# Gated cross-attention on one Trainium2 core: weights of the first batch split in other slots, from four staging places instead of two

## The reference

```
q = layernorm(x) @ Wq + bq            # 32 heads of 128
k, v = split(ctx @ Wkv + bkv)         # 8 heads of 128 each: four q heads share one
o = softmax(q k^T / sqrt(128)) v
x = x + tanh(g_xattn) * (o @ Wo + bo)
x = x + tanh(g_ffn) * ffn(layernorm(x))   # base matrix + 2 of 8 low-rank experts
```

## Time and profile before

| | us |
|---|---|
| three runs | 2407.01, 2410.34 (median), 2415.13 |
| the profiled execution, time | 2413.21 |
| the profiled execution, span from first to last instruction | 2411.1 |
| busy: TensorE / VectorE / ScalarE / GpSimd | 2305.1 / 1830.4 / 1687.1 / 1623.3 |
| mean granted TensorE clock | 0.984 |
| from one nm reduction to the next in the second batch (850.70, 884.34, 916.18, 950.79, 990.90 us) | 33.64, 31.84, 34.61, 40.11 |
| the same in the first batch (105.43, 147.39, 182.85, 220.53, 260.63 us) | 41.96, 35.46, 37.68, 40.10 |

### The profile page before, as it was taken

One profiled execution on the slowest core, in us unless ns is written; L12 is line 12 of the kernel. 1 busy time (PEld: TensorE's weight loads), 2 busy tenths in 40 slices (PEclk: granted clock), 3 DMA queues, 4 the chain that ended last, 5 costly groups with the idle time before them and its releaser, 6 DMA issues.

```text
span 2411.1 us, 37754 instructions
## 1 busy us (share of the span) xinstructions
PE 2305.1 (96%) x12568; PEld 1972.2 (82%) x12568; DVE 1830.4 (76%) x3167; ACT 1687.1 (70%) x3208; POOL 1623.3 (67%) x1367
## 2 busy tenths in 40 slices
PE   5889899899999999999999999999999999999988
PEld 5778788788888888888888888888888888888764
DVE  5677787778878777786877878787687878778775
ACT  4667676667767777776777777677677767777663
POOL 5687686876657767775776778577666747755652
PEclk9999999999999999999999999999999999999999
DMA  7333332336223233324213333333422222122201
GB/s 253 127 119 126 114 127 100 133 125 213 97 97 100 85 129 107 119 72 171 106 53 121 107 106 112 109 102 105 162 71 88 80 73 86 53 97 71 79 36 53
DMA packets 122591, 258.11 MB, mean 107 GB/s; under 512 B 13344, under 2 KB 46624, under 8 KB 122144
## 3 DMA queue, kind: packets, MB, share of 16 engines
q1 hardware_dynamic: 122400, 255.71, 31.4%
HBM read 188.81 MB, written 66.86 MB: 106 GB/s over the span
## 4 chain that ended last, share of the span: by engine, by line
PE 78%; POOL 7%; DVE 5%; issue 4%; DMA 4%; ACT 1%; SPq 1%; POOLq 0%; ACTq 0%; DVEq 0%
PE psW L350 11%; PE psW L351 11%; PE psW L352 11%; PE psW L533 7%; PE psW L535 7%; PE psW L534 7%; PE psS L350 6%; PE psS L352 6%; PE psS L351 6%; POOL xs L713 2%; DMA stg<-in_wq 2%; PE psW L405 2%; PE psW L413 2%; DVE mrun L1116 2%; PE psW L450 1%
## 5 line engine op out<-in xcount | busy, mean ns | idle before, releaser
L713 POOL TENSOR_TENSOR xs<-xs,mb 128x512 f32<-128x512 f32 (+1 forms) x832 | 1066.6, 1308 | 527.8 <-ACT mb L777 527.8
L1116 DVE TENSOR_TENSOR mrun<-psS,mrun 128x512 f32<-128x512 f32 (+1 forms) x704 | 484.1, 688 | 416.6 <-ACT xs L777 412.2
L777 ACT ACTIVATE xs<-psS 128x512 f32<-128x512 f32 (+1 forms) x832 | 497.6, 598 | 218.1 <-PE psS L352 208.7
L870 ACT ACTIVATE ph<-xs 128x512 fp32r<-128x512 f32 (+1 forms) x832 | 520.6, 626 | 0.0
L928 DVE TENSOR_TENSOR pl<-psP,ph 128x512 fp32r<-128x512 f32 (+1 forms) x674 | 460.9, 684 | 53.6 <-ACT ph L870 47.7
L1140 DVE TENSOR_TENSOR psum_<-psP,psum_ 128x512 f32<-128x512 f32 (+1 forms) x674 | 458.8, 681 | 20.7 <-POOL pl L717 20.7
L867 ACT ACTIVATE psP<-xs 128x512 f32<-128x512 f32 (+1 forms) x674 | 403.5, 599 | 1.7 <-DVE psum_ L1140 1.7
L533 PE MATMUL psW<-ph,vh 128*128 128x512 f32 (+1 forms) x832 | 338.6, 407 | 41.0 <-POOL pl L717 37.3
L350 PE MATMUL psS<-ql,kh 128*128 128x512 f32 (+1 forms) x832 | 345.8, 416 | 3.2 <-DVE mrun L1116 3.2
L535 PE MATMUL psW<-ph,vl 128*128 128x512 f32 (+1 forms) x832 | 330.0, 397 | 0.0
L534 PE MATMUL psW<-pl,vh 128*128 128x512 f32 (+1 forms) x832 | 329.9, 397 | 0.0
(11 more groups left out here) (145 smaller groups left out, 4580.5 us busy)
## 6 DMA issues: line engine op xcount, KB each, us to landing
wqh<-scr_wq SPq DMA_DIRECT2D x96, 256.0 KB, 2.7
wql<-scr_wq SPq DMA_DIRECT2D x96, 256.0 KB, 3.0
woh<-scr_wo SPq DMA_DIRECT2D x48, 512.0 KB, 3.3
wol<-scr_wo SPq DMA_DIRECT2D x48, 512.0 KB, 4.4
stg<-in_wq SPq DMA_DIRECT2D x32, 256.0 KB, 4.2
scr_wq<-wqh SPq DMA_DIRECT2D x32, 256.0 KB, 2.0
scr_wq<-wql SPq DMA_DIRECT2D x32, 256.0 KB, 2.5
stg<-in_wo SPq DMA_DIRECT2D x32, 256.0 KB, 3.2
```

Of the source, the lines that this page charges most:

```text
L713: eng.tensor_tensor(tile, tile, mb[0:rows_of(t), U % 2, :], ALU.subtract).then_inc(s_sub)
L777: return eng.activation(hi, src, ACT.Copy)
L870: eng.activation(ph[0:rows, T % RP, :], xs[0:rows, T % RX, :], ACT.Exp).then_inc(s_h)
L1116: eng.tensor_tensor(run, psS[0:rows, s % 2, :], a, ALU.max).then_inc(s_m)
```

## The change

It touches only what happens up to the end of the first batch. First, `cuts` is written by slots of the head and no longer by the projections; the number of splits is the same:

```
-            if kind == "q" and 2 * n + part + 2 < 2 * NU:
-                cuts[s + 1] += halves("q", 2 * n + part + 2)
-            if kind == "k" and part == 3 and n + 1 < 8:
-                cuts[s + 1] += halves("k", n + 1)
-            if kind == "v" and part == 12 and n + 1 < 4:
-                cuts[s + 1] += halves("v", n + 1)
-            if kind == "o" and part == 1 and n + 1 < NU:
-                cuts[s + 1] += halves("o", n + 1)
...
+    for U in range(NU + 1):
+        at, u = NT * U, U % 4
+        if U + 2 < NU:
+            cuts[at + 7] += halves("q", 2 * U + 4)
+            cuts[at + 8] += halves("q", 2 * U + 5)
+        if u % 2 == 0 and U // 2 + 1 < 8:
+            cuts[at + 9] += halves("k", U // 2 + 1)
+        if u == 3 and U // 4 + 1 < 4:
+            for a in range(2):
+                cuts[at + 9 + a].append(("v", U // 4 + 1, a))
+        if U != 1:
+            for a in range(2):
+                cuts[at + (12 if u == 3 or U == 0 else 13) + a].append(("o", max(U - 1, 0), a))
+        for t in (9, 11) if u == 1 else (11,) if u != 3 or U == 3 else ():
+            if spare:
+                cuts[at + t].append(spare.pop(0))
```

Second, four staging places: the two of stg, and until the last head of the batch the two of pp, which that batch doesn't use otherwise; a fetch may be issued ten slots ahead:

```
+        w = no % 4 if no < n4 else no % 2
+        last = there[w][-1] if there[w] else None
...
-            s = max(s, at - 5, cut_at[no - 2][1] + 1 if no - 2 >= len(first) else 0)
+            s = max(s, at - 10, cut_at[last][1] + 1)
...
+        def staged(no):
+            w = stage[no][0]
+            return stg[:, w, :] if w < 2 else pp[:, w - 2, :]
...
-                if no >= 2:
-                    sp.wait_ge(s_cut, 2 * (no - 1))
+                if last is not None:
+                    sp.wait_ge(s_cut, 2 * (last + 1))
...
+                        else:
+                            act.wait_ge(s_keep["c"], 32 * 16)
```

Third, GpSimd's steps in heads of the first batch:

```
-                "S0,S1 M,S2 L0,S3 S4 S5 S6 S7 S8 S9 S10 S11 S12 -",
+                "S0,S1 M,S2,S3 L0,S4 S5,S6 S7 S8 S9 S10 S11 S12 - - -",
```

```
+        for t, names in enumerate((AT[U % 4] if U else "k1 - k2 v0 q0 k3 q1 v1 - v2 - v3 -").split()):
...
-    jobs[0].append(("k", 0, 2))
...
-            proj_k(0, 1)
...
+                if c == 2:
+                    fetch("v", 0, 0)
+                    fetch("v", 0, 1)
+                    fetch("q", 2, 0)
+            fetch("q", 3, 0)
+            eng.dma_start(acc[:, :, :], x[:, 2:4, :]).then_inc(s_acc, 16)
...
-            upper_ctx(2)
-            upper_k(0, 1)
-            upper_ctx(3)
...
+                if s in (0, 2):
+                    upper_ctx(2 + s // 2)
...
-            lower_ctx(1)
             lower_k(0, 0)
             lower_q(0, 0)
             lower_q(0, 1)
-            lower_ctx(2)
-            lower_k(0, 1)
-            lower_ctx(3)
+            lower_ctx(1)
...
+                if s in (0, 2):
+                    lower_ctx(2 + s // 2)
```

More of the change, by code:

```diff
@@ L62, in gated_block @@
     for U in range(UN + 2):
-        for t, names in enumerate(AT[U % 4].split()):
+        for t, names in enumerate((AT[U % 4] if U else "k1 - k2 v0 q0 k3 q1 v1 - v2 - v3 -").split()):
             for name in names.split(","):
@@ L86, in gated_block @@
     cuts = {s: [] for s in range(SLOTS)}
-    for s in range(SLOTS):
-        for kind, n, part in jobs[s]:
-            if kind == "q" and 2 * n + part + 2 < 2 * NU:
-                cuts[s + 1] += halves("q", 2 * n + part + 2)
-            if kind == "k" and part == 3 and n + 1 < 8:
-                cuts[s + 1] += halves("k", n + 1)
-            if kind == "v" and part == 12 and n + 1 < 4:
-                cuts[s + 1] += halves("v", n + 1)
-            if kind == "o" and part == 1 and n + 1 < NU:
-                cuts[s + 1] += halves("o", n + 1)
-    cuts[0] += halves("q", 2) + halves("q", 3)
-    cuts[9] += halves("o", 0)
-    for n in range(16 * (B - 1)):
-        b, i = divmod(n, 16)
[L101 to L107, removed]
+    cuts[0] += halves("q", 2) + halves("q", 3)
+    spare = [("c", n, 0) for n in range(16)]
+    for U in range(NU + 1):
[14 more added lines that the diff above has]
+                cuts[at + t].append(spare.pop(0))
+    for n in range(16, 16 * (B - 1)):
+        b, i = divmod(n, 16)
+        cuts[NT * (NU * b + 3 + i // 2) + (10, 12)[i % 2]].append(("c", n, 0))
     cut_at = [(p, 0) for p in first] + [(p, s) for s in range(SLOTS) for p in cuts[s]]
@@ L111, in gated_block @@
     fetches = {s: [] for s in range(SLOTS)}
-    s = 0
+    stage, there, s = [], [[] for _ in range(4)], 0
     for no, (p, at) in enumerate(cut_at):
-        if no >= len(first):
-            s = max(s, at - 5, cut_at[no - 2][1] + 1 if no - 2 >= len(first) else 0)
+        n4 = sum(z < NT * (NU - 1) for _, z in cut_at)
+        w = no % 4 if no < n4 else no % 2
+        last = there[w][-1] if there[w] else None
+        stage.append((w, len(there[w]), last))
+        there[w].append(no)
+        if no >= len(first) + 2:
+            s = max(s, at - 10, cut_at[last][1] + 1)
+            assert s <= at, (p, at, s)
             fetches[s].append(p)
@@ L198, in gated_block @@
         s_in = {k: sem("s_in_" + k) for k in ("x", "wk", "c0", "c1", "c2", "c3")}
-        s_stg = [sem("s_stg0"), sem("s_stg1")]
+        s_stg = [sem("s_stg%d" % w) for w in range(4)]
         s_keep = {k: sem("s_keep_" + k) for k in ("q0", "q1", "k", "v", "o", "c")}
@@ L552, in fetch @@
                 no = number[kind, n, a]
-                if no >= 2:
-                    sp.wait_ge(s_cut, 2 * (no - 1))
-                    if order[no - 2][0] == "c":
-                        keep_ctx(order[no - 2][1])
-                        sp.wait_ge(s_keep["c"], 32 * (order[no - 2][1] + 1))
+                w, _, last = stage[no]
+                if last is not None:
+                    sp.wait_ge(s_cut, 2 * (last + 1))
+                    if order[last][0] == "c":
+                        keep_ctx(order[last][1])
+                        sp.wait_ge(s_keep["c"], 32 * (order[last][1] + 1))
                 if kind == "c":
-                    b, k, (lo, w) = n // 16 + 1, n % 4, CW[n // 4 % 4]
-                    eng.dma_start(stg[:, no % 2, 0:w], ctxT[b, :, k, lo:lo + w]).then_inc(s_stg[no % 2], 16)
+                    b, k, (lo, z) = n // 16 + 1, n % 4, CW[n // 4 % 4]
+                    eng.dma_start(staged(no)[:, 0:z], ctxT[b, :, k, lo:lo + z]).then_inc(s_stg[w], 16)
                 else:
-                    eng.dma_start(stg[:, no % 2, :], raw[kind](n, a)).then_inc(s_stg[no % 2], 16)
+                    eng.dma_start(staged(no), raw[kind](n, a)).then_inc(s_stg[w], 16)
             def keep(kind, n):
@@ L608, in _ @@
             eng.dma_start(bkv_sb[:, :], bkv).then_inc(s_c, 16)
+            eng.dma_start(tg[:, 0:1], gx.partition_broadcast(128)).then_inc(s_c, 16)
+            eng.dma_start(tg[:, 1:2], gf.partition_broadcast(128)).then_inc(s_c, 16)
             for c, (lo, w) in list(enumerate(CW))[1:]:
@@ L653, in _ @@
                     eng.dma_start(acc[:, :, :], scr_b[:, 2 * b:2 * b + 2, :]).then_inc(s_acc, 16)
[L654 to L659, removed]
+                if s in (5, 14, 22):
+                    r = (5, 14, 22).index(s) + 1
                     sp.wait_ge(s_bias, 2 * r)
                     eng.dma_start(scr_b[:, 2 * r:2 * r + 2, :], acc[:, :, :]).then_inc(s_sb, 16)
+                if s in (7, 16, 24):
+                    r = (7, 16, 24).index(s) + 1
+                    sp.wait_ge(s_sb, 16 * r)
+                    r = (r + 1) % 4
+                    eng.dma_start(acc[:, :, :], x[:, 2 * r:2 * r + 2, :]).then_inc(s_acc, 16)
                 if s == TN - 21:
@@ L686, in cut @@
                 no = number[kind, n, a]
-                raw = stg[:, no % 2, :]
+                raw = staged(no)
+                w, before, _ = stage[no]
                 if kind == "c":
-                    w = CW[n // 4 % 4][1]
-                    raw = raw[:, 0:w]
-                    hi, lo = cst[:, 0:w], raw
+                    z = CW[n // 4 % 4][1]
+                    raw = raw[:, 0:z]
+                    hi, lo = cst[:, 0:z], raw
                     if n:
@@ L702, in cut @@
                         pool.wait_ge(s_keep[name], 32 * i)
-                pool.wait_ge(s_stg[no % 2], 16 * (no // 2 + 1))
+                pool.wait_ge(s_stg[w], 16 * (before + 1))
                 eng.tensor_scalar(hi, raw, 1.0, 0.0, ALU.mult, ALU.add).then_inc(s_cut)
@@ L750, in _ @@
                     eng.tensor_scalar(xraw[:, :], xraw[:, :], tg[:, 0:1], None, ALU.mult).then_inc(s_bob)
-                if s in (4, 12, 20, 27):
-                    r = (s // 8 + 1) % 4
+                if s in (4, 13, 21, 28):
+                    r = (4, 13, 21, 28).index(s) + 1
                     pool.wait_ge(s_bob, 1)
-                    pool.wait_ge(s_acc, 16 * (s // 8 + 1))
-                    if r:
+                    pool.wait_ge(s_acc, 16 * r)
+                    if r < 4:
                         pool.wait_ge(s_bs, 2 + 2 * r)
@@ L902, in _ @@
```

(14 more changed lines are left out.)

2 lines of the change are left out of this document (1 added, 1 removed).

## The result

The changed kernel takes 2351.88 us (median of four runs, 2350.98 to 2352.85), the kernel before 2411.85 (2407.01 to 2415.13): ratio 0.9753, 95% interval 0.9735 to 0.9771. 2350 had been forecast. The profiled execution took 2350.98 us with a span of 2348.9, against 2413.21 and 2411.1.

A forecast was written before the change was run, and what follows sets the result against it. TensorE bounds the second batch; the first loses to its waits and lower clock. Gains of 43.5 us (heads 2 to 13), 12.5 (start) and 3.9 (second head) sum to 59.9, giving a median of 2350; 8-in-10 range 2343 to 2376.

The forecast's parts named there:

- The bound and the loss: First batch, heads 2 to 13: TensorE's idle time (30.0 us) and lower clock (13.5) vanish, worth 43.5 us, bounds 0 and 43.5.
- 15.5 us from 13.5: Lower clock in heads 2 to 13: 15.5 us by the clock column, 13.5 by the busy column; 13.5 was kept.
- Splits and subtractions: GpSimd, heads 2 to 13: mb to tile 0's low part takes 6.4 us instead of 14.9; nine TensorE waits go.
- The estimates of 3.1 and 1.3 us: Cover before TensorE would wait for GpSimd's low part: 3.1 us in head 6, some 1.3 us in the shortest heads.
- What is next in line: First batch's GpSimd: 114.28 us of load per four heads, not the bound; splits between subtractions 7 and 12 charged nothing.
- rival 3: GpSimd becomes the bound through splits between subtractions 7 and 12, so ScalarE's exponentials wait: 2432 us, chance 0.03.
- Four places: Staging in the first batch: pieces fetched up to ten slots ahead, asked for 3 to 14 slots before their split; cost nothing.
- x's rounds: Start of head 1: respaced loads and statistics of x shrink TensorE's 13.29 us idle to 0 to 3, 0.3 left.
- The lower bound of 8 us: Lowest gain claimed for the start, where 12.5 us was forecast with bounds 8 to 16.5.
- Head 0: Reordered first loads and first head: 0.5 us lost, bounds 3.2 gained and 3 lost, with three or four gaps of 1 to 2.
- the lost overlap that I had priced: Start: VectorE's half of a context chunk beside a GpSimd split costs 1.1 us more, expected at chunk 1 beside wq splits.
- Head 1: GpSimd's additions and context piece done earlier remove a 2.26 us wait and 1.6 us of clock: 3.9 us, bounds 0 and 3.9.

## Why the prediction was right

**The bound and the loss.** Forecast 43.5 us for heads 2 to 13, measured 44.7 by the maxima; of it some 2 us belong to head 1, because the maximum of head 1 now falls later within its slot (cut at the score matmuls of slots 15, 28 and 184, which are at 68.25, 106.80 and 570.93 before and at 57.01, 91.12 and 512.78 after, 42.5 us fall into these heads, 4.4 into head 1 and 11.2 ahead of it). The waits and the lower clock went together, as the earlier trace rows had them. The rounded clock column can't tell 15.5 us from 13.5: half a unit of its last digit over 464.13 us is 2.3 us. My reason for taking 13.5, that part of the lower clock lay on idle time, is not shown.

**Splits and subtractions.** The way from mb to the low part is the account, and its cover is 1.2 to 2.5 us from head 2 on and 0.28 us in head 1: shown by one half and by two halves of wo on that way. The estimates of 3.1 and 1.3 us were right for the short heads and 0.6 too long for head 6, since the low part waits 0.50 us for ScalarE's high part, which I had called covered.

**What is next in line.** The splits between subtractions 7 and 12 cost nothing (rival 3): no wait of ScalarE for a subtraction appears (the kernel before had six in heads 2 to 13, 8.1 us), and 115.5 us of work in 140.5 leave GpSimd early.

**Four places.** Priced at nothing for itself, and named as what ends the waits for pieces. The runs divide it further: in the changed kernel the places are worth 9.4 us, 9.05 of them in head 1; alone, on the kernel before, 40 us. A piece is asked for 3 to 10 slots ahead and not 3 to 14, as the edit `at - 10` says; the account doesn't hang on it. Slots and places are two ways to the same gain in the steady heads, where a late piece matters only between mb and the low part.

**x's rounds.** This step failed, though the sum did not. I took the 13.29 us as the price of the rounds' spacing, 13.0 of them to be gained by it. Alone it brings nothing (2414.50), undone it costs 1.3 us, which is within the noise. What held VectorE was GpSimd's addition behind a wq split that waited for its fetch, a context piece and k's split; the new slots move all three behind the addition. And whatever made VectorE early would have been handed to GpSimd's chain, which ended at nearly the same place, at 72.52. I had read that row for head 1's 2.26 us and not as the second end of the stall beside it. That the start came out near the forecast is luck in this respect: the gain was there, but another part of the change brought it. The lower bound of 8 us doesn't follow from its own terms either (13.3 - 3 - 3 = 7.3).

**Head 0.** Taken as 0.5 us lost, measured 2.6, inside the bounds of 3.2 gained to 3 lost. The gap is the one for chunk 2 (3.11 us), one of the three or four that I had seen but not priced one by one. Some 1.1 us of it are the lost overlap that I had priced, met by chunk 2 and not by chunk 1: half of chunk 2 takes VectorE 2.02 us (from 28.83), beside a wq split.

**Head 1.** Forecast 3.9 us; 3.85 by the score matmuls of slots 14 to 26 (33.31 us before, 29.46 after). From slot 15 to slot 28, a whole head, it is 4.4 us, above the bound of 3.9. The four places hold it in the changed kernel, where two places lose 9 us; with the old start and two places head 1 is only 1.3 us longer than in the changed kernel (36.18 against 34.88).

**The sum.** 59.9 forecast, 60.0 by the medians, but 58.15 in the two traces, where the start is 1.3 and the twelve heads 1.0 us below the forecast and head 1 0.5 above it. So the traces bear out 58 us, and that the medians agree with the forecast to 0.1 us is chance.

## What to carry to other kernels

An in-order engine that does background work must have it where no chain waits: find the moment from which each head's chain runs over it, subtract from the time at which the result is wanted, and keep background work out of that stretch; elsewhere it may even wait for its data. A stall at the start with one named releaser should be read for the second chain that ends beside it: if the next engine starts its next step at the same time for a reason of its own, removing the first alone gives nothing. And when two edits of one change can each do the job, test each alone before crediting either.

## What the runs showed of the hardware

The same wait is followed by a lower TensorE clock in one execution and not in the next, with nothing else changed. Two executions of the changed kernel, the stretch before and after TensorE's wait of 3.16 us for a maximum in the last batch (columns as above), first the repeat, then the first one:

```profile
2165.00:2176.00 11.00, 7.84 (x46) 6.87 (x45) 10.48 (x15) 6.73 (x15) 9.54 (x8) 1.00 0.13 46
2176.30:2179.70 3.40, 3.40 (x16) 3.25 (x15) 1.47 (x3) 1.62 (x4) 2.33 (x3) 0.50 0.00 0
```

```profile
2165.00:2176.00 11.00, 7.84 (x45) 6.91 (x44) 10.40 (x15) 6.74 (x15) 9.45 (x8) 1.00 0.12 45
2176.30:2179.70 3.40, 3.40 (x24) 2.95 (x23) 1.69 (x5) 2.63 (x6) 2.30 (x3) 1.00 0.10 25
```

16 matmuls at 1.2 GHz against 24 at 2.4 GHz in the same 3.4 us. In the fourteen profiled executions a lower clock follows this wait in eleven, a wait of some 2.25 us for GpSimd's low part near head 30 in ten, and a like one near head 46 in six. The price is read from the intervals between maxima: the one in the last batch is 43.53 to 43.56 us without the fall and 44.98 to 45.92 with it, so 1.4 to 2.4 us; the other two are 36.47 to 36.50 without and 37.08 to 38.04 with it, 0.6 to 1.6 us. The kernel with chunk 2 earlier had neither of the latter in its first profile and both in its second. The kernel before had all three, 0.87, 1.54 and 1.43 us, and the changed kernel's first profile had none: these 3.84 us are nearly all of the 4.05 us of the untouched part, and no gain of the change.
